# Cross attention on one core: four projections issued in halves between the heads

## The reference

```python
q = (x @ Wq).reshape(B, N, HEADS, hd).transpose(0, 2, 1, 3)
k = (context @ Wk).reshape(B, M, HEADS, hd).transpose(0, 2, 1, 3)
v = (context @ Wv).reshape(B, M, HEADS, hd).transpose(0, 2, 1, 3)
scores = jnp.einsum('bhid,bhjd->bhij', q, k) * scale
...
attn = jax.nn.softmax(scores, axis=-1)
out = jnp.einsum('bhij,bhjd->bhid', attn, v)
out = out.transpose(0, 2, 1, 3).reshape(B, N, DIM)
return out @ Wo
```

## Time and profile before

| | |
|---|---|
| median of 3 runs | 2955.56 us (2951.53 to 2962.2) |
| the profiled execution | 2948.41 us |
| its span, first to last instruction | 2946.5 us |
| mean granted TensorE clock | 0.879 |
| PE busy | 2322.9 us (79%) |
| PE weight loads busy | 1675.6 us (57%) |
| DVE busy | 1290.0 us (44%) |
| ACT busy | 1063.6 us (36%) |
| POOL busy | 616.9 us (21%) |

### The profile page before, as it was taken

One profiled execution on the slowest core, in us unless ns is written; L12 is line 12 of the kernel. 1 busy time (PEld: TensorE's weight loads), 2 busy tenths in 40 slices (PEclk: granted clock), 3 DMA queues, 4 the chain that ended last, 5 costly groups with the idle time before them and its releaser, 6 DMA issues. The chain is left out here.

```text
span 2946.5 us, 43378 instructions
## 1 busy us (share of the span) xinstructions
PE 2322.9 (79%) x13240; PEld 1675.6 (57%) x13241; DVE 1290.0 (44%) x2837; ACT 1063.6 (36%) x2491; POOL 616.9 (21%) x623
## 2 busy tenths in 40 slices
PE   2896298448799698889597897897999179838998
PEld 1564197224465474456375564467999156517887
DVE  3564200459665425956522564300000246465554
ACT  0464132214355422346531355213444035513332
POOL 0001200217521323722131000220000400023333
PEclk9798599669799798979797699898999569969999
DMA  6660332000000100000101672213220366200001
GB/s 197 116 119 12 128 130 87 27 26 0 10 0 3 44 1 26 0 10 0 47 1 35 116 123 37 77 53 125 79 110 18 88 119 123 43 13 27 22 21 34
DMA packets 119273, 165.65 MB, mean 56 GB/s; under 512 B 14394, under 2 KB 106269, under 8 KB 114045
## 3 DMA queue, kind: packets, MB, share of 16 engines
q1 hardware_dynamic: 113236, 150.64, 20.5%
q0 software_dynamic: 4608, 12.59, 1.3%
q10 hardware_dynamic: 1320, 1.03, 0.2%
HBM read 114.43 MB, written 47.32 MB: 55 GB/s over the span
## 5 line engine op out<-in xcount | busy, mean ns | idle before, releaser
L816 DVE TENSOR_REDUCE xa_mx<-ps 128x2 f32<-128x512 f32 x384 | 256.9, 690 | 221.3 <-PE ps L478 213.0
L668 ACT ACTIVATE xn_tok<-ps 128x512 f32<-128x512 f32 x384 | 227.4, 602 | 168.0 <-PE ps L486 166.4
L478 PE MATMUL ps<-xa_ks,xa_qs 48*128 48x256 f32 (+1 forms) x768 | 182.5, 349 | 47.6 <-DVE xa_mx L816 21.0
L1315 PE MATMUL ps<-ex_tiles,ex_w 128*128 x1792 | 213.2, 278 | 7.7 <-issue 4.2
L1315 PEld LDWEIGHTS ps<-ex_tiles,ex_w 128*128 128x128 f32 x1792 | 212.6, 195 | 11.3 <-issue 8.5
L1321 PE MATMUL ps<-ex_w,ex_h 128*128 128x256 f32 x896 | 202.7, 379 | 0.0
L478 PEld LDWEIGHTS ps<-xa_ks,xa_qs 48*128 48x128 f32 (+1 forms) x768 | 118.5, 208 | 137.5 <-issue 80.9
L1835 PE MATMUL ps<-lp_wqkv,lp_hs 128*128 128x512 f32 x384 | 176.4, 611 | 4.6 <-ACT lp_hs L1879 4.3
L1321 PEld LDWEIGHTS ps<-ex_w,ex_h 128*128 128x128 f32 x896 | 166.0, 190 | 20.2
L486 PE MATMUL ps<-xa_qs,xa_ks 49*128 49x256 f32 (+1 forms) x768 | 173.3, 332 | 0.7 <-ACT xn_tok L668 0.7
L1335 ACT ACTIVATE ex_h<-ps,ex_b 128x128 f32<-128x128 f32 x296 | 108.8, 368 | 152.8 <-PE ps L1315 132.7
(11 more groups left out here) (308 smaller groups left out, 5245.8 us busy)
## 6 DMA issues: line engine op xcount, KB each, us to landing
xa_ks<-x_keys SPq DMA_DIRECT2D x144, 128.0 KB
xa_qs<-x_queries SPq DMA_DIRECT2D x144, 128.0 KB, 4.3
ex_w<-in_L0f_w_dram SPq DMA_DIRECT2D x16, 1024.0 KB, 6.8
ex_w<-in_L2f_w_dram SPq DMA_DIRECT2D x16, 1024.0 KB, 6.3
x_keys<-xa_khl SPq DMA_DIRECT2D x24, 512.0 KB, 5.9
x_queries<-xa_qhl SPq DMA_DIRECT2D x24, 512.0 KB, 2.9
di_rows<-rows_in SPq DMA_DIRECT2D x16, 512.0 KB, 3.8
rows_out<-ex_tiles SPq DMA_DIRECT2D x62, 128.0 KB, 1.7
```

Source lines behind the costliest of these rows:

```text
L478: ins = nc.tensor.matmul(c.ps[:, M_BANK + h % 2, qt * S:(qt + 1) * S], qs[r:r + ROWS_M, b % Q_BUFS, n, qt * P:(qt + 1) * P], ks[r:r + ROWS ...
L668: nc.scalar.activation(pT[:, h % SLOTS].rearrange("p k q -> p (k q)"), c.ps[:, S_BANK + (HEADS * b + n) % 3], ACT.Exp).then_inc(exped.sem, 1)
L816: nc.vector.tensor_reduce(mx[:, half, :, col], c.ps[:, M_BANK + h % 2].rearrange("p (t n) -> p t n", t=2), AX_X, ALU.max).then_inc(max_put ...
L1315: ins = nc.tensor.matmul(c.ps[:, f % 4, 0:P], w1[:, par, k, f * P:(f + 1) * P], tile_of(n)[:, k], start=(k == 0), stop=(k == KD - 1))
```

## The change

Each of the four products is cut in two halves of 2 matmuls, and the halves stand after two steps. Where other work of the table and its readers stand moves too:

| work | block of step, before | now |
|---|---|---|
| `project_queries(b + 2)` | 4 | 3 and 4 |
| `turn_out(b - 1, 0)` | 4 | 5 |
| `weigh(b, 0)` | 5 | 6 |
| `turn_out(b - 1, 1)` | 6 | 7 |
| `project_keys(b + 3)` | 7 | 7 and 8 |
| `project_values(b + 1)` | 11 | 10 and 11 |
| `output(b - 1)` | 12 | 12 and 14 |
| ACT `put_rows(b + 2)` | 2 | 1 |
| ACT `lead_queries`, `put_o(b, 0)`, `lead_keys` | 4, 6, 8 | 5, 7, 9 |
| DVE `normalise_out(b - 1, 0)`, `(b - 1, 1)` | 5, 7 | 6, 8 |
| DVE `rest_keys(b + 3)` | 9 | 10 |
| DVE `add(b - 1)` | 13 | 15 |

Before batch 0, `project_keys(2)` stood after head 11 and now stands after heads 11 and 12. The core of the diff:

```diff
-            def project_values(b):
-                if b:
-                    pe.wait_ge(*k_rest(min(b + 3, B)))
-                pe.wait_ge(*q_rest(min(b + 2, B)))
-                pe.wait_ge(*v_put(b))
-                for kt in range(2):
+            def project_values(b, parts):
+                if parts[0] == 0:
+                    if b:
+                        pe.wait_ge(*k_rest(min(b + 3, B)))
+                    pe.wait_ge(*q_rest(min(b + 2, B)))
+                    pe.wait_ge(*v_put(b))
+                for kt in parts:
...
-                ins.then_inc(v_proj.sem, 1)
+                if kt:
+                    ins.then_inc(v_proj.sem, 1)
...
-                    elif n == 4:
+                    elif n == 3 or n == 4:
                         if b + 2 < B:
-                            project_queries(b + 2)
+                            project_queries(b + 2, n - 3)
+                    elif n == 5 and b:
+                        turn_out(b - 1, 0)
+                    elif n == 6:
+                        weigh(b, 0)
+                    elif n == 7:
                         if b:
-                            turn_out(b - 1, 0)
-                    elif n == 5:
-                        weigh(b, 0)
-                    elif n == 6 and b:
-                        turn_out(b - 1, 1)
-                    elif n == 7 and b + 3 < B:
-                        project_keys(b + 3)
+                            turn_out(b - 1, 1)
+                        if b + 3 < B:
+                            project_keys(b + 3, 0)
+                    elif n == 8 and b + 3 < B:
+                        project_keys(b + 3, 1)
                     elif n == 9:
                         if b + 1 < B:
                             turn_maxima(b + 1, 0)
                         weigh(b, 1)
-                    elif n == 10 and b:
-                        turn_back(b - 1)
+                    elif n == 10:
+                        if b:
+                            turn_back(b - 1)
+                        if b + 1 < B:
+                            project_values(b + 1, (0,))
                     elif n == 11 and b + 1 < B:
-                        project_values(b + 1)
+                        project_values(b + 1, (1,))
                     elif n == 12 and b:
-                        output(b - 1)
+                        output(b - 1, (0,))
                     elif n == 13:
                         weigh(b, 2)
+                    elif n == 14 and b:
+                        output(b - 1, (1,))
...
-                    if n == 5 and b:
-                        normalise_out(b - 1, 0)
-                    elif n == 6 and b + 2 < B:
-                        rest_queries(b + 2)
-                    elif n == 7 and b:
+                    if n == 6:
+                        if b:
+                            normalise_out(b - 1, 0)
+                        if b + 2 < B:
+                            rest_queries(b + 2)
+                    elif n == 8 and b:
                         normalise_out(b - 1, 1)
-                    elif n == 9 and b + 3 < B:
+                    elif n == 10 and b + 3 < B:
                         rest_keys(b + 3)
                     elif n == 11 and b + 3 < B:
                         normalise_rows(b + 3)
-                    elif n == 13 and b:
+                    elif n == 15 and b:
                         add(b - 1)
```

More of the change, by code:

```diff
@@ L444, in turn_rows @@
                 ins.then_inc(turned.sem, 1)
[L446 to L462, removed]
-            def project_values(b):
-                if b:
-                    pe.wait_ge(*k_rest(min(b + 3, B)))
-                pe.wait_ge(*q_rest(min(b + 2, B)))
-                pe.wait_ge(*v_put(b))
-                for kt in range(2):
+            def project_keys(b, part):
+                if part == 0:
+                    pe.wait_ge(*q_rest(b))
+                    if b == 2:
+                        pe.wait_ge(*v_put(1))
+                for k in range(KD):
+                    ins = nc.tensor.matmul(c.ps[:, W_BANK, part * S:(part + 1) * S], wk[:, k, part * P:(part + 1) * P],
+                                           c.ctxT[:, k, b * S:(b + 1) * S], start=(k == 0), stop=(k == KD - 1))
+                if part:
+                    ins.then_inc(k_proj.sem, 1)
@@ new lines, in project_queries @@
+            def project_queries(b, part):
+                if part == 0:
+                    pe.wait_ge(*x_put(b + 1))
+                for k in range(KD):
+                    ins = nc.tensor.matmul(c.ps[:, W_BANK, part * S:(part + 1) * S], wq[:, k, part * P:(part + 1) * P],
+                                           c.xT[:, k, b * S:(b + 1) * S], start=(k == 0), stop=(k == KD - 1))
+                if part:
+                    ins.then_inc(q_proj.sem, 1)
+            def project_values(b, parts):
[5 more added lines that the diff above has]
+                for kt in parts:
@@ L549, in turn_back, with output @@
                 ins.then_inc(on_turned.sem, 1)
-            def output(b):
+            def output(b, parts):
                 pe.wait_ge(*on_put(b + 1))
-                for qt in range(2):
+                for qt in parts:
                     for k in range(KD):
@@ L556, in output @@
                                                wo[:, k], start=(k == 0), stop=(k == KD - 1))
-                ins.then_inc(y_done.sem, 1)
+                if qt:
+                    ins.then_inc(y_done.sem, 1)
             pe.wait_ge(*loaded(16 * n_loads))
             pe.wait_ge(*mstep(MSTEPS))
-            project_keys(0)
+            project_keys(0, 0)
+            project_keys(0, 1)
             turn_rows(0)
-            project_queries(0)
-            project_keys(1)
+            project_queries(0, 0)
+            project_queries(0, 1)
+            project_keys(1, 0)
+            project_keys(1, 1)
             turn_rows(1)
-            project_queries(1)
+            project_queries(1, 0)
+            project_queries(1, 1)
             pe.wait_ge(*rows_set(16 * 2 * (1 + masked)))
@@ L570, in _ @@
                 if n == 4:
-                    project_values(0)
+                    project_values(0, (0, 1))
                 elif n == HALF:
                     turn_maxima(0, 0)
-                elif n == 11:
-                    project_keys(2)
+                elif n == 11 or n == 12:
+                    project_keys(2, n - 11)
             for b in range(B):
@@ L611, in _ @@
             turn_back(B - 1)
-            output(B - 1)
+            output(B - 1, (0, 1))
         @block.scalar
@@ L705, in _ @@
                     if n == 1:
+                        if b + 2 < B:
+                            put_rows(b + 2)
                         put_maxima(b, 1)
@@ L708, in _ @@
                         send_maxima(b, 1)
-                        if b + 2 < B:
-                            put_rows(b + 2)
                     elif n == 3 and b:
@@ L714, in _ @@
                         top_queries(b, 1)
-                        if b + 2 < B:
-                            lead_queries(b + 2)
-                    elif n == 6:
+                    elif n == 5 and b + 2 < B:
+                        lead_queries(b + 2)
+                    elif n == 7:
                         put_o(b, 0)
[L719 to L722, removed]
+                    elif n == 9:
+                        if b + 3 < B:
+                            lead_keys(b + 3)
+                        if b + 1 < B:
+                            put_maxima(b + 1, 0)
                     elif n == 10:
@@ L726, in _ @@
                         put_o(b, 1)
-                    elif n == 11:
-                        if b:
-                            put_back(b - 1)
+                    elif n == 11 and b:
+                        put_back(b - 1)
                     elif n == 12 and b + 1 < B:
```

## The result

The changed kernel takes 3000.12 us (median of 4 runs, 2990.54 to 3020.56), the kernel before, measured beside it, 2953.77. The ratio is 1.0161, 95% interval 1.0104 to 1.0217. The direction was the forecast one; the size, +46 us instead of +17.6, lies outside the range. The profiled execution has a span of 2998.9 us (before 2946.5), so +52.4 us, and a mean granted clock of 0.869 (0.879).

What follows compares the result with a forecast made beforehand. PE was taken to bound the kernel. Terms of +21.6 us (batches 1 to 4), +3.0 (batch 5), +2.4 (batches 6 and 7) and -9.4 (clock) sum to +17.6, giving 2973 us against the median, range 2952 to 2992.

Steps and rivals of the forecast that it cites:

- More runs: Batches 1 to 4: three new runs of other work between PE's steps cost 0.4 us each, +1.2 us a batch.
- A new wait for `k_rest`: Step 10, batches 1 to 4: the values' projection waits for DVE's moved `rest_keys`, +1.0 us a batch.
- Waits that shrink: Batches 1 to 4: PE's waits for `rest_queries` and at step 0 shrink, -0.2 us each.
- Batch 0 and the clock: Batch 0's moves give 0; the shorter maxima DMA wait keeps the clock up in batch 1, -9.4 us in all.
- the first rival: The clock falls as before, from the DMA wait or step 10's new wait: 2983 us; 0.32 including worse.
- Batches 6 and 7 get one run more each: 6 x 0.4 = +2.4.: Last two batches of each cross attention: one new run each, +2.4 us in all.
- falls elsewhere too: New 1 us waits let the clock fall elsewhere, 3.1 us each; three falls give 2992 us; within the 0.32.
- nearly a draw: Passages between step and block are waits, new runs cost nothing, the `k_rest` wait stays: 2953 us; 0.19 with its halfway.
- faster: PE's waits for DVE go, the clock recovers, new runs cost nothing: -22 us, 2934 us; chance 0.11.

Runs made afterwards that it cites:

- E6: The kernel before with only the queries' projection in halves behind heads 3 and 4, `put_rows` at 1; batches 2 to 4 take 22.66 us instead of 22.26.
- E3: The changed kernel with `rest_keys` back behind the maximum of head 9 instead of head 10; 1.0135 of the time before.
- E1: The changed kernel with batches 6 and 7 put back to the order of before; 1.0050 of the time before.
- E2: The changed kernel with only batch 7 put back to the order of before; 1.0111 of the time before.
- E4: The kernel before with the change's order in batch 0 alone of each cross attention; 1.0009 of the time before.
- E5: The changed kernel with the `add` of batch 6 behind the maximum of head 14 instead of 15; 1.0063 of the time before.
- E9: The changed kernel again, unaltered, on another chip; 1.0135 of the time before.
- E15: The changed kernel with `add` of batch 6 behind the maximum of head 14, a repeat of E5; no ratio given.
- E7: The kernel before, nothing halved, with only `add` moved behind the maximum of head 15; 1.0042 of the time before.
- E10: The order of before built from the changed source, for a second profile; tails 66.7, 69.5 and 65.7 us.
- E16: The kernel before with only `add` behind the maximum of head 15, a repeat of E7; no ratio given.

## Why the prediction was right and wrong

- *More runs, 0.4 each:* right. E6 measures 0.40. A half as a block takes 1.06 (forecast 1.07), a step with it 1.50, in PE in order of time of the changed kernel, batch 4:

```profile
190.88 0.38 PE L482 MATMUL ps<-xa_ks,xa_qs 49*128 49x256 f32 x1
...
191.32 1.13 PE L461 MATMUL ps<-xn_T,xa_wq 128*128 128x256 f32 x4
192.38 0.38 PE L482 MATMUL ps<-xa_ks,xa_qs 49*128 49x256 f32 x1
...
200.74 0.66 PE L551 MATMUL ps<-ident,xa_on 128*128 128x128 f32 x4
202.24 1.13 PE L475 MATMUL ps<-xa_wv,ctx_T 128*128 128x256 f32 x4 [0.85 <-DVE xa_khl L812]
...
209.88 0.66 PE L442 MATMUL ps<-ident,xa_row 128*128 128x128 f32 x4
210.50 0.38 PE L482 MATMUL ps<-xa_ks,xa_qs 49*128 49x256 f32 x1
...
211.18 0.41 PE L519 MATMUL ps<-ident,xa_mx 128*128 128x128 f32 x2 [0.18 <-DVE x_res L853]
```

- *A new wait for `k_rest`, 1.0 us:* right. It is 0.85 (202.24), and DVE in order of time shows the order that makes it. E3 takes it away and the batch loses 1.0.

```profile
200.84 0.69 DVE L833 TENSOR_REDUCE xa_mx<-ps 128x2 f32<-128x512 f32 x1 [1.16 <-PE ps L482]
201.45 0.74 DVE L812 SCALAR_TENSOR_TENSOR xa_khl<-ps,xa_anyk,xa_khl 128x512 fp32r<-128x512 f32 x1
```

- *Waits that shrink, -0.4:* too small. `rest_queries` is no longer waited for (0.26), and step 0 not at all, with 0.18 at `turn_maxima` instead of 0.77. For batch 4 that makes 1.2 + 0.85 - 0.26 - 0.77 + 0.18 = +1.2, and +1.2 is measured; on average over batches 2 to 4 it is +1.5 against the forecast 1.8. Batch 3 has 0.3 us more before the step 0 that ends it, which I didn't resolve.
- *Batch 0 and the clock:* the maxima's DMA isn't waited for any more, step 0 waits 0.7 (forecast 0.9), and the clock stays up in batch 1. Batch 0 itself got 0.7 to 2.0 us shorter where I said 0: I had walked it from step 10 on. In the first cross attention the keys' projection waits 0.31 us for `rest_queries` in step 7 instead of 1.14. That the clock stayed up in all three is luck in part. The new wait for `k_rest` is the 1.5 us in batch 0 that the first rival named, here in PE's list of the changed kernel:

```profile
109.27 1.13 PE L475 MATMUL ps<-xa_wv,ctx_T 128*128 128x256 f32 x4 [1.44 <-DVE xa_khl L812]
```

  In the seven kernels with this order in batch 0 (the change, E1, E2, E4, E5, E9, E15) a fall begins 1.2 to 1.4 us behind the end of it in 8 of 21 cross attentions, and in two of E9's three. Over the three cross attentions batches 0 and 1 together changed by -11.4 us in the profile of the change against the one before. The six profiles with the change in both batches have 146.1 us on average for them, the five with both as before (before, E6, E7, E10, E16) 148.6: -2.5, where -4.0 was forecast.
- *"Batches 6 and 7 get one run more each: 6 x 0.4 = +2.4."* This is the step that failed, by what it left out. I priced `add` behind head 15 at 0.1 us for `turn_maxima` by walking a batch in which a `turn_rows` and full steps lie between them. At the turn from batch 6 to 7 there is neither, and the wait is 1.23 us. That itself is cheap, 3.7 us in all. But mostly the clock falls with it, and in the tail it stays down for up to 36 us in one piece. The rival "falls elsewhere too" priced a fall at the 3.1 us of batch 1. Measured: tails of +35.7 instead of +5.4 us, of which the experiments give some 21 to the place of one `add`, and 9 (three times the 2.9 of E5 and E15) to everything else that the change does in a tail. The rest of the +52.4, with the 12.3 outside the cross attentions, is not assigned; the profiles scatter by as much.
- *The rivals:* nearly a draw and faster both rested on passages that cost nothing; E6 excludes that. The rival in which waits let the clock fall elsewhere too had the mechanism, with another wait (`k_rest`) and too low a price.

What stays open: why the clock falls behind this wait in most tails and not in all, and why it comes back late. Nor is the length of the wait all that counts: behind the 1.44 us in batch 0 the clock fell less often (8 of 21) than behind 0.85 in batch 7 (4 of 6, few as they are). The normalised results of batches 5 and 6 are now waited for by `turn_maxima` as well (6.5 us in 6 waits, 1.3 the longest), also in E5 and E15. Behind the one of about 1.25 us in batch 6 falls begin too, in 12 of the 24 tails of kernels that have it and in none of the 30 others, but they lasted 3 to 7 us. Not tried: halves of the tail with all its waits removed.

## What to carry to other kernels

Walk a moved instruction through the first and the last rounds of a pipeline too, not only through the middle: where neighbours drop out, a wait of 0.1 us becomes 1.2. Price a wait on an engine whose clock can fall by what the clock does after it, here 7 us on average for a wait of 0.85 to 1.23. And count the passages between matmuls of different tile shapes before cutting a block in two: 0.40 us each here, more than the waits that the halves took away.

## What the runs showed of the hardware

- A passage from steps that use 49 or 50 rows of the array to full blocks and back costs 0.40 us at the full clock, in PE's busy time (E6: 21.58 against 21.18), while the weight loads' row names a maximum of DVE.
- The clock, once at 0.5 in a tail, stayed there for 36 us (the change, first and third cross attention) although PE was busy for 31.56 of 37.63 us; falls that began in batches 0 to 4 lasted 3 to 17 us, all but five of them at most 10. At one and the same place it fell in some executions and not in others (E7: 0, 10 and 53 us of half clock in three tails).
- Behind a wait of 0.85 to 1.23 us at the turn from batch 6 to 7 the clock fell in 15 of 21 tails, behind one of 0.16 to 0.72 us there in none of 33.
- The layers that no kernel here changes took from 2334 to 2376 us in the profiles: a part of the span must be compared, not the whole.
